# Third attention: its three layer norms applied by ScalarE instead of VectorE, their bias made by GpSimd, second statistics issued behind the division

## The chip, the cores and the metric

One NeuronCore of a Trainium2 chip runs the whole program. The metric is the device time of one execution in microseconds (us). The engines are TensorE (PE, matmuls and weight loads), VectorE (DVE), ScalarE (ACT), GpSimd (POOL) and the DMA queues, which are fed here by SyncE (SP). Each engine takes its own instructions in order; between engines only semaphores order the work.

## What is computed

The network is four residual blocks one after another on 16 sequences of 256 tokens with 128 channels (4096 tokens): a Mamba block, an attention with a mixture of experts, the window attention this change is about, and a two-layer local attention. The third one is

```
x = x + layernorm(attn(layernorm(x)))          # no learned scale or shift in these norms
attn: q, k, v of x; windows of 32 tokens every 16 (8 windows for the 128 + 16 tokens used of a sequence),
      per head of 8 channels scores over the channels' window axis, softmax, output projection W_out
layernorm(x) = (x - mean) / sqrt(var + 1e-5)
```

The local attention that follows starts with a layer norm of this block's result, so the phase ends with yet another norm: for each group of tokens it leaves both x3 = x + norm(attention) and r = norm(x3).

## The kernel before

The program is five phases, each a block with one instruction list per engine; a block ends with a barrier of all engines. The phase of this change is `phase_windows` (from L1953). It has a head and a loop.

**Head.** `x` arrives as 18 tiles of 128 tokens x 128 channels, handled as three sets of six tiles (`norm(k)`, L2192). For each set VectorE takes the statistics (`bn_stats`, `bn_aggr`), adds epsilon into `ve` (L2201), waits for GpSimd, which raises `ve` to the power of -0.5 into `rstd` (L2042), and then applies the norm itself, one `tensor_scalar` per tile, (x - mean) * rstd (L2204). TensorE transposes the normed tiles (`turn_x`, L2057), ScalarE copies them out of PSUM (`copy_x`, L2147), TensorE makes values (`values`) and queries and keys (`queries_keys`), ScalarE copies the values with their bias (`copy_v`), and VectorE adds the bias to queries and keys (`bias(b)`, L2207, 16 sequences). VectorE's written order is norm 0, norm 1, bias 0 to 3, norm 2, bias 4 to 15.

**Loop.** A group is two sequences; there are 8 groups (NG = 8), and each has a turn in which TensorE does, in this order, `weigh(g)` (128 small matmuls of attention weights with values, L2110), `scores(g + 2)` (128 small matmuls, L2094; none for g = 6 and 7) and `project(g)` (L2119, the output projection into the single PSUM bank `y_ps`). `project(g)` waits for two things of VectorE: the transposed heads of its own group (`oT_rd`) and that the bank has been read for the group before (`at_least(pe, y_rd, g)`, L2117).
VectorE's order in the loop is written out by hand (L2287 to L2301):

```
for g in range(NG + 2):
    if g < NG:          turn(g)              # transpose weights, row sums, reciprocal
    if 2 <= g:          first_norm(g - 2)    # yn = (y - mean) * rstd, 4 tiles (L2254)
    if g + 1 < NG:      shift(g + 1)         # add mask, maximum, subtract it
    if 2 <= g:          second_stats(g - 2)  # waits for GpSimd's x3 (L2271)
    if g < NG:          divide(g)            # waits for weigh(g); multiply (L2236), transpose (L2241)
    if 1 <= g <= NG:    take(g - 1)          # reads y_ps (L2260), statistics of y
    if 2 <= g:          second_norm(g - 2)   # ro = (x3 - mean) * rstd, 4 tiles (L2254)
```

ScalarE has only the exponentials here (`exps(g)`, L2166). GpSimd does for each group `rstd1` (L2045), x3 = yn + xr (L2049) and `rstd2` (L2051). SP sends x3 and r of each group out and fetches them into the next phase's tiles. `at_least(engine, semaphore, n)` is a wait that is left out for n = 0; `then_inc` is the signal at an instruction's end; `ln.mark` and `ln.settle` are VectorE's waits for its own instructions.

Of the kernel before, what the change touches and what calls it, by code (L numbers as in the profile page):

```python
# [14 lines left out]
P = 128  # L15
# [10 lines left out]
def at_least(eng, sem, value):  # L26

    if not isinstance(value, int) or value > 0:
        eng.wait_ge(sem, value)
# [1923 lines left out]
def phase_windows(nc, resident, old, signals, x2_dram, x3_dram, r_dram, t):  # L1953
# [8 lines left out]
    with ExitStack() as ctx:  # L1962
# [3 lines left out]
        mhalf = m.sb("mhalf", [P, 6])  # L1966
        xt = m.sb("xt", [P, NT, C])
        stat, mv = m.sb("stat", [P, 6, 6]), m.sb("mv", [P, 6, 2])
        ve, rstd = m.sb("ve", [P, 6]), m.sb("rstd", [P, 6])
        xn = m.sb("xn", [P, NT, C])  # L1970
        xT = m.sb("xT", [P, NB, WTOK])
        vT = m.sb("vT", [P, NB, WTOK])
# [5 lines left out]
        xr = [m.sb(f"xr{i}", [P, NCH, C]) for i in range(2)]  # L1978
        y = m.sb("y", [P, NCH, C])
        stat1, mv1, stat2, mv2 = (m.sb(n, [P, NCH, k]) for n, k in (("stat1", 6), ("mv1", 2), ("stat2", 6), ("mv2", 2)))  # L1980
        ve1, rstd1, ve2, rstd2 = (m.sb(n, [P, NCH]) for n in ("ve1", "rstd1", "ve2", "rstd2"))
        yn = m.sb("yn", [P, NCH, C])
        xo = [m.sb(f"xo{i}", [P, NCH, C]) for i in range(2)]
        ro = [m.sb(f"ro{i}", [P, NCH, C]) for i in range(2)]
# [16 lines left out]
        def tiles_of(k):  # L2001

            return [16, 17, 0, 1, 2, 3] if k == 0 else list(range(6 * k - 2, 6 * k + 4))
# [5 lines left out]
        with nc.Block() as block:  # L2009
# [26 lines left out]
            @block.gpsimd  # L2036
            def _(pool):
                clear(pool, old)
                pool.wait_ge(w_rd, 1)
                for k in range(3):  # L2040
                    pool.wait_ge(var_rd, k + 1)
                    nc.gpsimd.tensor_tensor(rstd[:, :], ve[:, :], mhalf[:, :], ALU.pow).then_inc(rstd_rd, 1)  # L2042
                for g in range(NG):
                    pool.wait_ge(var1_rd, g + 1)
                    nc.gpsimd.tensor_tensor(rstd1[:, :], ve1[:, :], mhalf[:, 0:NCH], ALU.pow).then_inc(rstd1_rd, 1)  # L2045
                    pool.wait_ge(yn_rd, g + 1)
                    pool.wait_ge(r_in[g % 2], 16 * (g // 2 + 1))
                    at_least(pool, x_out[g % 2], 32 * (g // 2))
                    nc.gpsimd.tensor_tensor(xo[g % 2][:, :, :], yn[:, :, :], xr[g % 2][:, :, :], ALU.add).then_inc(x3_rd, 1)  # L2049
                    pool.wait_ge(var2_rd, g + 1)  # L2050
                    nc.gpsimd.tensor_tensor(rstd2[:, :], ve2[:, :], mhalf[:, 0:NCH], ALU.pow).then_inc(rstd2_rd, 1)  # L2051

            @block.tensor
            def _(pe):
# [90 lines left out]
            @block.scalar  # L2145
            def _(act):
                def copy_x(k):  # L2147
                    for i, tiles in enumerate(banks(k)):
                        act.wait_ge(xT_mm, 2 * k + i + 1)
                        if tiles[0] >= NB:  # L2150
                            ins = nc.scalar.copy(xT[:, :, P:WTOK], t_ps[i][:, 0:2 * P].rearrange("p (b t) -> p b t", t=TAIL))
                        else:
                            ins = nc.scalar.copy(xT[:, tiles[0]:tiles[-1] + 1, 0:P],
                                                 t_ps[i][:, 0:len(tiles) * P].rearrange("p (b t) -> p b t", t=P))
                        ins.then_inc(xT_sb, 1)

                def copy_v(n):
                    b0, b1 = 3 * n, min(3 * n + 3, NB)
                    act.wait_ge(v_mm, n + 1)
                    nc.scalar.activation(vT[:, b0:b1, :].rearrange("p b t -> p (b t)"), (o_ps, y_ps)[n % 2][:, 0:(b1 - b0) * WTOK],  # L2160
                                         ACT.Identity, bias=bv[:, 0:1]).then_inc(v_sb, 1)

                def exps(g):
                    act.wait_ge(sub_rd, g + 1)
                    at_least(act, aT_rd, g)
                    nc.scalar.activation(at[:, :, :], sc[:, :, :], ACT.Exp).then_inc(ex_rd, 1)  # L2166

                act.wait_ge(w_rd, 1)
                copy_x(0)
                copy_v(0)  # L2170
                copy_x(1)
                copy_v(1)
                copy_v(2)
                copy_x(2)
                for n in range(3, 6):
                    copy_v(n)
                for g in range(NG):
                    exps(g)

            @block.vector  # L2180
            def _(dve):
# [10 lines left out]
                def norm(k):  # L2192
                    tiles = tiles_of(k)
                    dve.wait_ge(x_in[k], 16 * (20 if k == 0 else 6))
                    for c, b in enumerate(tiles):
                        ln.mark(dve.bn_stats(stat[:, c, :], xt[:, b, :]))
                    ln.settle(apart=True)
                    for c in range(6):
                        ln.mark(dve.bn_aggr(mv[:, c, :], stat[:, c, :]))
                    ln.settle()  # L2200
                    dve.tensor_scalar(ve[:, :], mv[:, :, 1], EPS, None, ALU.add).then_inc(var_rd, 1)  # L2201
                    dve.wait_ge(rstd_rd, k + 1)
                    for c, b in enumerate(tiles):
                        ins = dve.tensor_scalar(xn[:, b, :], xt[:, b, :], mv[:, c, 0:1], rstd[:, c:c + 1], ALU.subtract, ALU.mult)  # L2204
                    ins.then_inc(xn_rd, 1)

                def bias(b):  # L2207
                    dve.wait_ge(qk_mm, b + 1)
# [3 lines left out]
                def shift(g):  # L2212
                    dve.wait_ge(s_mm, g + 1)
                    at_least(dve, ex_rd, g)
                    dve.tensor_tensor(sc[:, :, :].rearrange("p (i j) t -> p i (j t)", i=4), s_all[:, :, 0:P],
                                      off[:, :].unsqueeze(1).to_broadcast([P, 4, P]), ALU.add).then_inc(sc_rd, 1)
                    dve.wait_ge(sc_rd, g + 1)
                    dve.tensor_reduce(nb[:, :], sc[:, :, :], AX.X, ALU.max).then_inc(nb_rd, 1)
                    dve.wait_ge(nb_rd, g + 1)
                    dve.tensor_tensor(sc[:, :, :], sc[:, :, :], nb[:, :].unsqueeze(2).to_broadcast([P, 4 * SQ * 2, WIN]),  # L2220
                                      ALU.subtract).then_inc(sub_rd, 1)
# [18 lines left out]
                    at_least(dve, y_mm, g)  # L2240
                    dve.transpose(oT[:, :, :, :].rearrange("p h k d -> p k h d"), on[:, :, :]).then_inc(oT_rd, 1)  # L2241

                def stats(src, st, mean, dst, done):
                    for c in range(NCH):
                        ln.mark(dve.bn_stats(st[:, c, :], src[:, c, :]))
                    ln.settle(apart=True)
                    for c in range(NCH):
                        ln.mark(dve.bn_aggr(mean[:, c, :], st[:, c, :]))
                    ln.settle()
                    dve.tensor_scalar(dst[:, :], mean[:, :, 1], EPS, None, ALU.add).then_inc(done, 1)  # L2250

                def apply(dst, src, mean, r):
                    for c in range(NCH):
                        ins = dve.tensor_scalar(dst[:, c, :], src[:, c, :], mean[:, c, 0:1], r[:, c:c + 1], ALU.subtract, ALU.mult)  # L2254
                    return ins

                def take(g):
                    dve.wait_ge(y_mm, g + 1)
                    at_least(dve, yn_rd, g)
                    dve.tensor_tensor(y[:, :, :], y_ps[:, :].rearrange("p (c n) -> p c n", c=NCH),  # L2260
                                      bo[:, :].unsqueeze(1).to_broadcast([P, NCH, C]), ALU.add).then_inc(y_rd, 1)
                    dve.wait_ge(y_rd, g + 1)
                    stats(y, stat1, mv1, ve1, var1_rd)

                def first_norm(g):
                    dve.wait_ge(rstd1_rd, g + 1)
                    at_least(dve, x3_rd, g)
                    apply(yn, y, mv1, rstd1).then_inc(yn_rd, 1)

                def second_stats(g):  # L2270
                    dve.wait_ge(x3_rd, g + 1)  # L2271
                    stats(xo[g % 2], stat2, mv2, ve2, var2_rd)

                def second_norm(g):
                    dve.wait_ge(rstd2_rd, g + 1)
                    at_least(dve, x_out[g % 2], 32 * (g // 2))
                    apply(ro[g % 2], xo[g % 2], mv2, rstd2).then_inc(ro_rd, 1)

                norm(0)
                norm(1)  # L2280
# [6 lines left out]
                for g in range(NG + 2):  # L2287
                    if g < NG:
                        turn(g)
                    if 2 <= g:  # L2290
                        first_norm(g - 2)
                    if g + 1 < NG:
                        shift(g + 1)
                    if 2 <= g:
                        second_stats(g - 2)
                    if g < NG:
                        divide(g)
                    if 1 <= g <= NG:
                        take(g - 1)
                    if 2 <= g:  # L2300
                        second_norm(g - 2)  # L2301


    return m.sems
# [860 lines left out]
```

## Time and profile before

| | us |
|---|---|
| median of 3 runs (lowest, highest) | 2429.15 (2426.51, 2434.3) |
| the profiled execution, its own time | 2433.53 |
| its span | 2431.6 |
| TensorE busy | 1976.8 (81%) |
| VectorE busy | 1865.4 (77%) |
| ScalarE busy | 1331.8 (55%) |
| GpSimd busy | 689.4 (28%) |
| mean granted TensorE clock | 0.917 |

The phase of the change lies from about 1301 to 1446 us of that span, some 145 us. Times in the rows are microseconds from the span's start, `[2.43 <-issue]` behind a row is idle time of the engine before it and what ended it ("issue": nothing that the profile shows). A row of several instructions (x4) gives their first start and the time from there that they cover. Busy shares are means over the whole program, so the rows that matter are those of this phase.

### The profile page before, as it was taken

How to read it: one execution, taken by the hardware profiler on the slowest of the kernel's cores; microseconds unless marked ns; L12 is line 12 of the kernel's file. 1: busy time of each engine (PE TensorE's matmuls, PEld its weight loads, DVE VectorE, ACT ScalarE, POOL GpSimd, SP SyncE). 2: the span in 40 equal slices, each digit the busy share in tenths (PEclk: the TensorE clock that was granted, in tenths of full speed). 3: DMA queues.
4: the chain of work that ended last, by engine and by line, in shares of the span. 5: the costliest groups of instructions: out<-in, count | busy, mean ns of one | idle time of the engine just before them, and what ended most of it. 6: DMA issues, size and time to landing. Idle time of an engine off the chain costs nothing. (4 is left out here: it accounts for less than half of the span.)

```text
span 2431.6 us, 39165 instructions
## 1 busy us (share of the span) xinstructions
PE 1976.8 (81%) x12768; PEld 1080.7 (44%) x12768; DVE 1865.4 (77%) x4483; ACT 1331.8 (55%) x2870; POOL 689.4 (28%) x598
## 2 busy tenths in 40 slices
PE   5787787786488989876952758999999999999985
PEld 2233332332234444443422425565656556666553
DVE  5999999999567777741235778888886788888865
ACT  5665656764124444433432007787885487878731
POOL 1333334323201222222441143333331233333211
PEclk8999888998779999978985879999999999999997
DMA  8000000000121111103334130000000000000000
GB/s 282 3 1 5 5 5 5 0 5 5 27 81 36 38 40 39 40 23 107 97 103 135 47 122 1 1 1 1 1 1 1 1 1 1 1 1 2 1 13 22
DMA packets 76458, 79.20 MB, mean 33 GB/s; under 512 B 10004, under 2 KB 60735, under 8 KB 75264
## 3 DMA queue, kind: packets, MB, share of 16 engines
q1 hardware_dynamic: 72160, 68.64, 9.6%
q0 software_dynamic: 4096, 8.06, 1.0%
q8 instruction: 104, 1.70, 0.3%
q14 instruction: 98, 0.80, 0.1%
HBM read 39.19 MB, written 37.85 MB: 32 GB/s over the span
## 5 line engine op out<-in xcount | busy, mean ns | idle before, releaser
L768 DVE TENSOR_TENSOR_SCAN m_hs<-m_da,m_bu 128x1024 f32<-128x1024 f32 x128 | 304.6, 2419 | 0.3
L465 PE MATMUL m_ps_y_ps<-m_prod,m_ident 128*128 128x512 f32 x512 | 278.8, 672 | 4.9 <-DVE m_prod L778 4.9
L1324 ACT ACTIVATE a_pt<-a_ps_s 128x1024 f32<-128x1024 f32 x128 | 131.0, 1024 | 230.1 <-PE a_ps_s L1102 230.1
L375 POOL TENSOR_TENSOR m_bu<-m_dtu,m_bsb 128x1024 f32<-128x1024 f32 x64 | 151.3, 2364 | 366.2 <-ACT m_bsb L616 233.3
L2795 ACT ACTIVATE l_pe<-l_ps_s,l_nbias,l_qs 128x192 f32<-128x192 f32 (+1 forms) x512 | 244.4, 487 | 14.1 <-DVE l_nbias L2963 12.1
L1441 DVE TENSOR_REDUCE a_mpad<-a_ps_s 128x4 f32<-128x1024 f32 x128 | 156.8, 1225 | 94.3 <-PE a_ps_s L1094 93.1
L1094 PE MATMUL a_ps_s<-a_heads 32*128 32x256 f32 x1024 | 188.0, 447 | 45.3 <-DVE a_mpad L1441 29.0
L1102 PE MATMUL a_ps_s<-a_qm,a_heads 32*128 32x256 f32 x1024 | 186.3, 441 | 1.6 <-ACT a_pt L1324 1.2
L2551 PE MATMUL l_ps_s<-l_kT,l_qT 128*128 128x384 f32 (+1 forms) x512 | 180.2, 434 | 0.0
L625 ACT ACTIVATE m_da<-m_dt,m_a_neg 128x510 f32<-128x510 f32 x256 | 167.9, 714 | 3.2 <-DVE m_hs L768 1.7
L465 PEld LDWEIGHTS m_ps_y_ps<-m_prod,m_ident 128*128 128x128 f32 x512 | 113.2, 221 | 113.9 <-issue 97.2
L2805 ACT COPY l_pT<-l_ps_t 128x256 f32<-128x256 f32 (+1 forms) x256 | 122.7, 479 | 72.9 <-PE l_ps_t L2561 45.8
L778 DVE TENSOR_TENSOR m_prod<-m_hs,m_ps_c_ps 128x1024 f32<-128x1024 f32 x128 | 153.9, 1203 | 10.1 <-PE m_ps_y_ps L465 9.7
L616 ACT COPY m_bsb<-m_ps_b_ps 128x512 f32<-128x512 f32 x64 | 37.4, 584 | 209.3 <-PE m_ps_b_ps L451 209.1
L2515 PE MATMUL l_ps_qk<-t_wqkv,l_hT 128*128 128x512 f32 x256 | 145.4, 652 | 1.8 <-ACT l_hT L2755 0.8
L1094 PEld LDWEIGHTS a_ps_s<-a_heads 32*128 32x128 f32 x1024 | 82.3, 193 | 131.5 <-PE a_ps_s L1102 60.3
L2975 DVE TENSOR_SCALAR l_pn<-l_pe,l_ri 128x192 f32<-128x192 f32 (+1 forms) x512 | 132.3, 300 | 10.0 <-DVE l_ri L2971 1.2
L456 PE MATMUL m_ps_c_ps<-m_bc,m_sel 96*128 96x512 bf16 x128 | 54.9, 430 | 99.1 <-DVE m_prod L778 99.1
L2960 DVE TENSOR_REDUCE l_top<-l_ps_s 128x2 f32<-128x256 f32 (+1 forms) x256 | 123.9, 484 | 12.0 <-PE l_ps_s L2551 8.6
L2579 PE MATMUL l_ps_o<-l_pT,l_v 128*64 128x128 f32 x1024 | 113.3, 297 | 12.5 <-ACT l_oT L2811 9.8
L2561 PE MATMUL l_ps_t<-t_ident,l_pn 128*128 128x128 f32 x512 | 100.1, 277 | 26.5 <-DVE l_pn L2975 26.5
L1028 POOL TENSOR_TENSOR a_rstd<-a_ve,a_mhalf 128x2 f32<-128x2 f32 x48 | 33.8, 704 | 306.6 <-DVE a_ve L1399 164.8
(330 smaller groups left out, 4706.2 us busy)
## 6 DMA issues: line engine op xcount, KB each, us to landing
slots<-m_void SPq DMA_DIRECT2D x16, 516.0 KB, 6.3
e_xs<-slots SPq DMA_DIRECT2D x16, 258.0 KB, 2.8
ys<-m_void SPq DMA_DIRECT2D x8, 512.0 KB, 6.7
qk<-a_qk SPq DMA_DIRECT2D x16, 256.0 KB, 2.0
a_heads<-qk SPq DMA_DIRECT2D x64, 64.0 KB
ew_w<-in_w SPq DMA_DIRECT2D x2, 2048.0 KB, 12.5
e_yy<-ys SPq DMA_DIRECT2D x16, 256.0 KB, 5.3
m_xt<-in_L_attn_x SPq DMA_DIRECT2D x8, 256.0 KB, 3.2
```

The source lines that it names most:

```text
L375: nc.gpsimd.tensor_tensor(bu[s % 4][:, :, :], dtu[p][:, :, :], b2, ALU.mult).then_inc(bu_rd, 1)
L465: last = pe.matmul(y_ps[h][:, :], ident[:, :], prod[s % 2][:, h, :], start=False, stop=(s == NS - 1))
L625: nc.scalar.activation(da[s % 4][:, h, :, 1:], dt[p][:, h, :, 1:], ACT.Exp, scale=a_neg[:, h, s:s + 1]).then_inc(da_rd, 1)
L768: dve.tensor_tensor_scan(hs[s % 2][:, :, :].rearrange("p h t -> p (h t)"), da[s % 4][:, :, :, :].rearrange("p h q t -> p (h q t)"), bu[s % ...
L778: dve.tensor_tensor(prod[s % 2][:, :, :], hs[s % 2][:, :, :], c2, ALU.mult).then_inc(prod_rd, 1)
L1094: last = pe.matmul(dst[:, j, :], qT[p][r, g, c * P:(c + 1) * P], kT[p][r, g, :], start=True, stop=True)
L1102: last = pe.matmul(s2[:, j, :], kT[p][r, g, c * P:(c + 1) * P], qm[p][r, g, :], start=True, stop=True)
L1441: dve.tensor_reduce(dst, src[:, :, :], AX.X, ALU.max, negate=True).then_inc(max_rd, 1)
L2515: pe.matmul(qk_ps[:, x, :], hT[:, c * P:(c + 1) * P], t.wqkv[n][:, x * INNER:(x + 1) * INNER], start=True, stop=True).then_inc(l.x_mm[x], 1)
L2551: pe.matmul(both, qT[p][:, j, c * P:(c + 1) * P], kT[p][:, :, j, k0:k0 + nk], start=False, stop=True).then_inc(l.s_mm, 1)
L2795: nc.scalar.activation(pe_[u % 2][:, h, 0:nk], s_ps[u % 2][:, h * 192:h * 192 + nk], ACT.Exp, bias=nbias[:, u % 2, h:h + 1], scale=qs[b % ...
L2975: ins = dve.tensor_scalar(pn[u % 2][:, h, 256 - nk:256], pe_[u % 2][:, h, 0:nk], ri[:, h:h + 1], None, ALU.mult)
```

## The change

GpSimd makes, beside each `rstd`, the product `sh` = (-mean) * rstd, with one more small multiply that waits for the power before it. VectorE writes -mean (`nm`) next to `ve` and no longer applies any norm. ScalarE applies all three norms as Identity with a scale and a bias for each partition, one activation per tile: six per set in the head, four per group for the first and for the second norm. In the head it does so in the order norm 0, copy 0, norm 1, values 0, copy 1, norm 2, values 1 and 2, copy 2. In the loop it does first norm of g - 2, exponentials of g + 1, second norm of g - 2. VectorE's loop becomes turn, shift, divide, second_stats, take. New waits protect the single buffers: GpSimd's power waits for ScalarE's use of the one before, VectorE's statistics wait for GpSimd's use of the mean.

```diff
@@ GpSimd
                 for k in range(3):
                     pool.wait_ge(var_rd, k + 1)
+                    at_least(pool, xn_rd, k)
                     nc.gpsimd.tensor_tensor(rstd[:, :], ve[:, :], mhalf[:, :], ALU.pow).then_inc(rstd_rd, 1)
+                    pool.wait_ge(rstd_rd, 2 * k + 1)
+                    nc.gpsimd.tensor_tensor(sh[:, :], nm[:, :], rstd[:, :], ALU.mult).then_inc(rstd_rd, 1)
                 for g in range(NG):
                     pool.wait_ge(var1_rd, g + 1)
+                    at_least(pool, yn_rd, g)
                     nc.gpsimd.tensor_tensor(rstd1[:, :], ve1[:, :], mhalf[:, 0:NCH], ALU.pow).then_inc(rstd1_rd, 1)
+                    pool.wait_ge(rstd1_rd, 2 * g + 1)
+                    nc.gpsimd.tensor_tensor(sh1[:, :], nm1[:, :], rstd1[:, :], ALU.mult).then_inc(rstd1_rd, 1)
                     pool.wait_ge(yn_rd, g + 1)
...
                     pool.wait_ge(var2_rd, g + 1)
+                    at_least(pool, ro_rd, g)
                     nc.gpsimd.tensor_tensor(rstd2[:, :], ve2[:, :], mhalf[:, 0:NCH], ALU.pow).then_inc(rstd2_rd, 1)
+                    pool.wait_ge(rstd2_rd, 2 * g + 1)
+                    nc.gpsimd.tensor_tensor(sh2[:, :], nm2[:, :], rstd2[:, :], ALU.mult).then_inc(rstd2_rd, 1)
@@ ScalarE
+                def normalise(dst, src, scale, shift, n):
+                    for c in range(n):
+                        ins = nc.scalar.activation(dst[c], src[c], ACT.Identity, bias=shift[:, c:c + 1], scale=scale[:, c:c + 1])
+                    return ins
+
+                def norm_x(k):
+                    act.wait_ge(rstd_rd, 2 * (k + 1))
+                    tiles = tiles_of(k)
+                    normalise([xn[:, b, :] for b in tiles], [xt[:, b, :] for b in tiles], rstd, sh, 6).then_inc(xn_rd, 1)
+
+                def first_norm(g):
+                    act.wait_ge(rstd1_rd, 2 * (g + 1))
+                    at_least(act, x3_rd, g)
+                    normalise([yn[:, c, :] for c in range(NCH)], [y[:, c, :] for c in range(NCH)], rstd1, sh1, NCH).then_inc(yn_rd, 1)
+
+                def second_norm(g):
+                    p = g % 2
+                    act.wait_ge(rstd2_rd, 2 * (g + 1))
+                    at_least(act, x_out[p], 32 * (g // 2))
+                    normalise([ro[p][:, c, :] for c in range(NCH)], [xo[p][:, c, :] for c in range(NCH)], rstd2, sh2, NCH).then_inc(ro_rd, 1)
...
                 act.wait_ge(w_rd, 1)
+                norm_x(0)
                 copy_x(0)
+                norm_x(1)
                 copy_v(0)
                 copy_x(1)
+                norm_x(2)
                 copy_v(1)
                 copy_v(2)
                 copy_x(2)
                 for n in range(3, 6):
                     copy_v(n)
-                for g in range(NG):
-                    exps(g)
+                exps(0)
+                for g in range(NG + 2):
+                    if 2 <= g:
+                        first_norm(g - 2)
+                    if g + 1 < NG:
+                        exps(g + 1)
+                    if 2 <= g:
+                        second_norm(g - 2)
@@ VectorE, head
                     ln.settle(apart=True)
+                    at_least(dve, rstd_rd, 2 * k)
                     for c in range(6):
                         ln.mark(dve.bn_aggr(mv[:, c, :], stat[:, c, :]))
                     ln.settle()
+                    dve.tensor_scalar(nm[:, :], mv[:, :, 0], -1.0, None, ALU.mult)
                     dve.tensor_scalar(ve[:, :], mv[:, :, 1], EPS, None, ALU.add).then_inc(var_rd, 1)
-                    dve.wait_ge(rstd_rd, k + 1)
-                    for c, b in enumerate(tiles):
-                        ins = dve.tensor_scalar(xn[:, b, :], xt[:, b, :], mv[:, c, 0:1], rstd[:, c:c + 1], ALU.subtract, ALU.mult)
-                    ins.then_inc(xn_rd, 1)
@@ VectorE, loop: stats() likewise gains the wait, nm1 or nm2; apply(), first_norm() and second_norm() go
                 for g in range(NG + 2):
                     if g < NG:
                         turn(g)
-                    if 2 <= g:
-                        first_norm(g - 2)
                     if g + 1 < NG:
                         shift(g + 1)
+                    if g < NG:
+                        divide(g)
                     if 2 <= g:
                         second_stats(g - 2)
-                    if g < NG:
-                        divide(g)
                     if 1 <= g <= NG:
                         take(g - 1)
-                    if 2 <= g:
-                        second_norm(g - 2)
```

## Rows read from the trace of the kernel before

**Rows 1.** Windows view, one loop turn: us, busy per engine (count), clock, DMA share, GB/s
```profile
1387.50:1398.00 10.50, 7.72 (x265) 4.47 (x265) 10.05 (x36) 0.63 (x1) 3.33 (x4) 0.83 0.41 128
```
**Rows 2.** Timeline, PE, turns 1 to 3: start, us, engine, line, op, names, count [idle]
```profile
1361.63 1.25 PE L2110 MATMUL w_ps_o<-w_vT,w_aT 32*32 32x32 f32 x126
...
1371.72 1.25 PE L2110 MATMUL w_ps_o<-w_vT,w_aT 32*32 32x32 f32 x126
...
1376.47 0.42 PE L2094 MATMUL w_ps_s<-w_qk 32*32 32x32 f32 x31 [2.64 <-issue]
...
1376.82 5.25 PE L2119 MATMUL w_ps_y<-aw_xn,w_oT 128*128 128x512 f32 x8
...
1381.99 1.25 PE L2110 MATMUL w_ps_o<-w_vT,w_aT 32*32 32x32 f32 x126
```
**Rows 3.** Timeline, DVE: the division of turn 1, then part of turn 3
```profile
1363.02 0.69 DVE L2236 TENSOR_TENSOR w_on<-w_ps_o,w_ri 128x512 f32<-128x512 f32 x1 [4.15 <-PE w_ps_o L2110]
...
1382.11 0.86 DVE L2245 BATCH_NORM_STATS2 w_stat<-w_xo 128x6 f32<-128x128 f32 x4
...
1383.60 0.69 DVE L2236 TENSOR_TENSOR w_on<-w_ps_o,w_ri 128x512 f32<-128x512 f32 x1
...
1384.96 0.65 DVE L2260 TENSOR_TENSOR w_y<-w_ps_y,aw_xn 128x512 f32<-128x512 f32 x1
...
1387.04 0.17 DVE L2250 TENSOR_SCALAR w_ve<-w_mv 128x4 f32<-128x4 f32 x1
```
**Rows 4.** Timeline, PE and DVE, turns 6 and 7
```profile
1412.78 1.29 PE L2110 MATMUL w_ps_o<-w_vT,w_aT 32*32 32x32 f32 x128
...
1415.38 0.69 DVE L2236 TENSOR_TENSOR w_on<-w_ps_o,w_ri 128x512 f32<-128x512 f32 x1
...
1416.75 0.65 DVE L2260 TENSOR_TENSOR w_y<-w_ps_y,aw_xn 128x512 f32<-128x512 f32 x1
...
1417.55 5.35 PE L2119 MATMUL w_ps_y<-aw_xn,w_oT 128*128 128x512 f32 x8 [3.48 <-DVE w_y L2260]
...
1422.82 1.29 PE L2110 MATMUL w_ps_o<-w_vT,w_aT 32*32 32x32 f32 x128
...
1425.31 0.69 DVE L2236 TENSOR_TENSOR w_on<-w_ps_o,w_ri 128x512 f32<-128x512 f32 x1
```
**Rows 5.** Timeline, DVE and POOL, from the last turn to the end of the phase
```profile
1431.27 1.26 POOL L2049 TENSOR_TENSOR w_xo<-w_yn,w_xr 128x512 f32<-128x512 f32 x1 [1.23 <-DVE w_yn L2254]
...
1432.57 0.87 DVE L2245 BATCH_NORM_STATS2 w_stat<-w_xo 128x6 f32<-128x128 f32 x4 [1.38 <-POOL w_xo L2049]
...
1434.03 0.69 DVE L2260 TENSOR_TENSOR w_y<-w_ps_y,aw_xn 128x512 f32<-128x512 f32 x1
...
1442.65 1.11 DVE L2254 TENSOR_SCALAR w_ro<-w_xo,w_mv,w_rstd 128x128 f32<-128x128 f32 x4 [1.13 <-POOL w_rstd L2051]
```
**Rows 6.** Timeline, head of the phase: set 0, then set 2 and queries and keys
```profile
1313.60 0.17 DVE L2201 TENSOR_SCALAR w_ve<-w_mv 128x6 f32<-128x6 f32 x1
1313.92 1.32 POOL L2042 TENSOR_TENSOR w_rstd<-w_ve,w_mhalf 128x6 f32<-128x6 f32 x1 [18.38 <-DVE w_ve L2201]
1315.28 1.63 DVE L2204 TENSOR_SCALAR w_xn<-w_xt,w_mv,w_rstd 128x128 f32<-128x128 f32 x6 [1.51 <-POOL w_rstd L2042]
...
1329.23 0.17 DVE L2201 TENSOR_SCALAR w_ve<-w_mv 128x6 f32<-128x6 f32 x1
...
1329.63 5.55 PE L2079 MATMUL w_ps_s<-aw_xn,w_xT 128*128 128x256 f32 x24
...
```
**Rows 7.** Timeline, ACT, phase before: four tiles with scale and bias
```profile
1295.78 1.65 ACT L1810 ACTIVATE e_yy<-e_yy,e_shift,e_rstd 128x128 f32<-128x128 f32 x4 [1.71 <-DVE e_shift L1927]
```
**Rows 8.** Source views of L2045, L358 (min/median/max ns), and DVE beside L358
```profile
L2045 POOL TENSOR_TENSOR w_rstd<-w_ve,w_mhalf x8: 1007/1042/1045, 1366.7 to 1436.4; 128x4 f32<-128x4 f32 x8
...
L358 POOL TENSOR_TENSOR m_shift_in<-m_nmean,m_rstd x8: 199/3897/3906, 6.6 to 461.5; 128x4 f32<-128x4 f32 x8
...
310.09 4.46 DVE L768 TENSOR_TENSOR_SCAN m_hs<-m_da,m_bu 128x1024 f32<-128x1024 f32 x2
```

More of the change, by code:

```diff
@@ L1968, in phase_windows @@
         stat, mv = m.sb("stat", [P, 6, 6]), m.sb("mv", [P, 6, 2])
-        ve, rstd = m.sb("ve", [P, 6]), m.sb("rstd", [P, 6])
+        ve, rstd, sh = (m.sb(n, [P, 6]) for n in ("ve", "rstd", "sh"))
+        nm, nm1, nm2 = m.sb("nm", [P, 6]), m.sb("nm1", [P, NCH]), m.sb("nm2", [P, NCH])
         xn = m.sb("xn", [P, NT, C])
@@ L1980, in phase_windows @@
         stat1, mv1, stat2, mv2 = (m.sb(n, [P, NCH, k]) for n, k in (("stat1", 6), ("mv1", 2), ("stat2", 6), ("mv2", 2)))
-        ve1, rstd1, ve2, rstd2 = (m.sb(n, [P, NCH]) for n in ("ve1", "rstd1", "ve2", "rstd2"))
+        ve1, rstd1, sh1, ve2, rstd2, sh2 = (m.sb(n, [P, NCH]) for n in ("ve1", "rstd1", "sh1", "ve2", "rstd2", "sh2"))
         yn = m.sb("yn", [P, NCH, C])
@@ L2241, in divide, with stats @@
                     dve.transpose(oT[:, :, :, :].rearrange("p h k d -> p k h d"), on[:, :, :]).then_inc(oT_rd, 1)
-                def stats(src, st, mean, dst, done):
+                def stats(g, src, st, mean, less, dst, done, used):
                     for c in range(NCH):
@@ L2246, in stats @@
                     ln.settle(apart=True)
+                    at_least(dve, used, 2 * g)
                     for c in range(NCH):
@@ L2249, in stats @@
                     ln.settle()
+                    dve.tensor_scalar(less[:, :], mean[:, :, 0], -1.0, None, ALU.mult)
                     dve.tensor_scalar(dst[:, :], mean[:, :, 1], EPS, None, ALU.add).then_inc(done, 1)
[L2252 to L2255, printed above, removed]
                 def take(g):
@@ L2262, in take @@
                     dve.wait_ge(y_rd, g + 1)
[L2263 to L2268, printed above, removed]
+                    stats(g, y, stat1, mv1, nm1, ve1, var1_rd, rstd1_rd)
                 def second_stats(g):
                     dve.wait_ge(x3_rd, g + 1)
[L2272 to L2277, printed above, removed]
+                    stats(g, xo[g % 2], stat2, mv2, nm2, ve2, var2_rd, rstd2_rd)
                 norm(0)
```

## The prediction

> **What bounds the kernel now.** The share of busy time says little here, since this phase is 145 of 2432 us. I read first the windows view, one window per turn of the loop: a turn lasts 10.5 us and VectorE is busy for 10.05 of it [rows 1]. That invites the reading that VectorE is the bound and that whatever is taken from it is gained. The timeline of TensorE says otherwise. The weighs of turns 1, 2 and 3 start at 1361.63, 1371.72 and 1381.99, so 10.09 and 10.27 us apart [rows 2], and in the first of these two intervals VectorE sat idle for 4.15 us waiting for the weigh [rows 3]: with VectorE plainly not the limit, the pitch was already the same. What fills it is TensorE's own list: the weigh of 1.25 us, the scores with a hole of 2.64 us that no semaphore explains, and the projection of 5.25 us at 1376.82, which ends as the next weigh starts [rows 2]. Through turn 5 VectorE (10.5 us a turn) runs just behind TensorE (10.1 to 10.3) and eats its slack without yet stopping it. Only in turns 6 and 7, which have no scores, does TensorE wait for VectorE: the projection starts at 1417.55 behind 3.48 us of idling, released by VectorE's read of the bank `y_ps` [rows 4]. After turn 7 the phase is one serial chain through VectorE and GpSimd to the last second norm [rows 5], and in the head everything stands behind the first normed set [rows 6].
>
> So there are four places: head, turns 2 to 5, turns 6 and 7, tail.
>
> **Prices of the new pieces.** ScalarE's norm of four tiles: the same operation on the same shape, Identity with scale and bias, took 1.65 us in the phase before [rows 7], and I take 1.65 for four, 0.41 a tile, 2.48 for six. VectorE needs 1.11 us for four and 1.63 for six [rows 5, 6]. GpSimd's multiply of 128x4 exists in the Mamba phase, from 0.20 us up to 3.90, the long ones under VectorE's scans [rows 8]. The single operations of VectorE in these rows take 0.7 us at most, and in the tail it waits while GpSimd multiplies, so I take 0.20 plus 0.08 for the step from the power, the gap seen from `ve` to the power; 3.90 stays as the upper end. The extra `nm` on VectorE: between 0.02 and the 0.17 us of its twin `ve` [rows 3]; as neighbours on VectorE start before the one before is reported done, I take 0.09. A handover from GpSimd to ScalarE is priced as that from GpSimd to VectorE, 0.04 [rows 6].
>
> A rule speaks against the move. The Trainium skill, page "ScalarE: Activation LUTs", in its closing table of situations, gives add and multiply to VectorE, up to about three times faster there in bf16. The trace has the same direction but 1.5 times for fp32. With that factor of three instead, a four-tile norm would cost 3.3 us, and the estimate below would grow by about 1.7 for each of three norms and 2.4 for the head, to about 12 us.
>
> **Head.** Before, from the end of `ve` (1313.77) to the end of set 0's norm (1316.91) it is 3.14 us [rows 6]. After: 0.15 to the power, 1.32, then 0.28 for the multiply, 0.04, and 2.48 on ScalarE, 4.27 in all: +1.1 us, and TensorE's transposes wait for the last tile. From there to the scores TensorE's list is nearly unbroken, so the delay reaches the loop; a few tenths may return, because VectorE no longer norms set 2 while banks wait to be read, and these I leave to the lower edge. ScalarE's `norm_x(2)` stands ahead of `copy_v(1)` and `copy_v(2)`, but those have no user before set 2 is transposed: with `ve` of set 2 at 1329.40 + 1.1 and 4.27 behind it, the norm ends at about 1334.8, and TensorE is done with queries and keys 4 to 9 at 1335.18 + 1.1 [rows 6]. The work beside it hides it. Head: +1.1.
>
> **Turns 2 to 5.** VectorE loses 2 x 1.11 us of norms and gains 2 x 0.09. This frees VectorE, not TensorE. But the new order has a cost of its own: `take`, whose first instruction reads the bank that `project(g)` waits for, now stands behind the second statistics, which stand behind the division. Counted from a weigh's start: the division starts 1.39 later [rows 2, 3], the transpose and it take 1.36 to the next instruction (1383.60 to 1384.96), the statistics 1.46 (1432.57 to 1434.03) [rows 3, 5] and `nm` 0.09, so the bank's read starts at 4.30; 0.65 to read and 0.15 to reach TensorE [rows 4] give 5.10. Before, the projection started 5.10 after its weigh [rows 2]. The wait is thus just hidden by the hole in the scores: 0, at most 0.1 a turn. Are the second statistics' inputs there? `take` ends 2.25 + 0.09 after 4.30, at 6.64. Then 0.08 + 1.04 power [rows 8], 0.28 multiply, 0.04, 1.65 ScalarE, 0.08 + 1.26 GpSimd's add and 0.04: 4.47, so x3 is there at 11.11, which is 0.9 after the next weigh, and is wanted at 2.75. Slack 1.85. ScalarE has the exponentials between its two norms; it is free by then. Sum: +0.05.
>
> **Turns 6 and 7.** The division came late, 2.60 and 2.49 after the weigh instead of 1.39 [rows 4], and that is repaired. It gives nothing, since the projection waits for the bank: before, the bank was read straight after the division and the projection started 4.77 after weigh 6 [rows 4]; now it is 5.10. Weigh 7 comes +0.33 later. Turn 7 loses the like, but that is covered by the tail's own wait.
>
> **Tail.** `take(7)` stands behind the second statistics of group 6, as before. Their input comes 11.11 after weigh 7 by the chain above, and 1.55 later the bank is read: 12.66. Before it was 1434.03 - 1422.82 = 11.21 [rows 4, 5]: +1.45. The projection itself is done at about 10.5, so it hides nothing. Behind it both norms of group 7 are serial: twice 0.28 for the multiply, 0.09 for `nm` and 1.65 - 1.11 = 0.54 for ScalarE, +1.8. The output DMA, SP's two fetches and the barrier follow the last norm, so all of it reaches the end.
>
> **Sum:** 1.1 + 0.05 + 0.33 + 1.45 + 1.8 = 4.7 us slower. The profiled execution took 2433.53 (span 2431.6); it would take 2438. It lay 4.4 above the median of the runs, 2429.15, from which I forecast 2433.9. That is 0.19%, below the 0.3% (7.3 us) which is about what a measurement of this kernel can tell from no change. With the multiply at 0.2 to 0.7 and `nm` at 0.02 to 0.17 the case spans +3.5 to +8, and with the spread of the runs shown 2430 to 2439.
>
> **Rivals.**
> (1) *VectorE is the bound after all, and the loop gets its time back.* For it: 10.05 of 10.5 us busy, and the late divisions. Then turns 2 to 7 gain 2.22 - 0.18 = 2.04 each, 12.2 us, against 1.1 + 1.45 + 1.8: 8 us faster, 2421. It decides if TensorE's turn can be under 10.1, that is if the hole in its scores shrinks and the bank's wait too. Against it stands the pitch of 10.09 beside 4.15 us of VectorE idling, and the new cycle weigh, division, second statistics, read, projection, which is 5.10 + 5.2 whatever else is gained. Chance 0.07.
> (2) *The multiply on GpSimd is held up by VectorE.* In the Mamba phase the same multiply took 3.90 us while two scans of VectorE ran over it [rows 8]. The Trainium skill, "GPSIMD Engine Reference", Key points, says that GpSimd shares its SBUF interfaces with VectorE and contends with VectorE's two-input or two-port instructions. Here the subtraction in `shift` is of that kind, once a turn. The case decides when the multiply takes over 0.2 + 1.85 us: then x3 is late, VectorE waits in the second statistics, the bank is read late and TensorE's projection with it. At 3.90 that is 3.70 - 1.85 = 1.85 in each of turns 2 to 7, 11.1 us, and 3.7 in the head: +19, 2448, slower. Against it: the eight powers of the first norms stay between 1.01 and 1.05 us [rows 8], beside a busy VectorE as beside an idle one, and no scan runs. Chance 0.08.
> (3) *The change's parts cancel.* If the hand-overs and the multiply are all at their lower ends and the head's delay is caught up by TensorE before the loop, 1 to 2 us remain, 2431. It is the lower edge of my case, inside its chance.
>
> **Numbers.** My case has 0.85, of which about a fifth reaches over +7.3 us (bank wait of 0.1 to 0.3 in every turn, or handovers to ScalarE dearer than to VectorE). Faster: 0.07. Slower: 0.08 + 0.17 = 0.25. Same: 0.68. The range leaves out rival 1 and most of rival 2: 2428.5 to 2440.5.
>
> **What would show it.** In the changed trace: the first transposes about 1.1 us later; pitch of the weighs in turns 2 to 5 unchanged within 0.2 while VectorE now idles one to two us a turn; the projections of turns 6 and 7 released by L2260's counterpart at about 5.1 after their weighs; the read of the bank for group 7 at about 12.7 after weigh 7; the phase 4 to 5 us longer. A pitch under 10 us would prove the sum wrong on one side, GpSimd multiplies of over 1 us on the other.

## The result and the profile after

| | before | after |
|---|---|---|
| median of 20 runs each (lowest, highest), us | 2428.76 (2422.19, 2434.88) | 2436.72 (2429.23, 2440.45) |
| ratio, 95% interval | | 1.0026 (1.0018 to 1.0034), so +4.4 to +8.3 us |
| the phase of the change, VectorE's first instruction in it to its first in the next | 144.5 | 149.1 |
| VectorE busy, ScalarE busy, GpSimd busy, us | 1865.4, 1331.8, 689.4 | 1846.3, 1364.8, 694.8 |

The forecast was +4.7 us, 2433.9, within the 0.3% that counts as no change; measured is +6.3 by the ratio (the medians lie 8.0 apart). VectorE lost 19 us of work and the program became slower. The two profiled executions differ by less, 1.2 us in their spans, because in the second the phases ahead of this one happened to take 3.2 us less; so the whole is read from the 20 runs and the phase from its own start. In the changed kernel the weigh is L2120, the projection L2129, the division L2274, the bank's read L2295, ScalarE's norms L2175.

The windows view of one turn of the changed kernel, columns as in [rows 1]:
```profile
1385.00:1395.50 10.50, 8.00 (x265) 4.54 (x265) 8.34 (x31) 3.92 (x9) 4.01 (x6) 0.83 0.40 129
```
VectorE is busy 8.34 us of the turn where it was 10.05 [rows 1]; TensorE's 8.00 stands against 7.72. The turn did not get shorter. The timeline of turns 5 to 7 answers to [rows 2] and [rows 4]:
```profile
1400.43 1.25 PE L2120 MATMUL w_ps_o<-w_vT,w_aT 32*32 32x32 f32 x126
...
1405.51 5.32 PE L2129 MATMUL w_ps_y<-aw_xn,w_oT 128*128 128x512 f32 x8 [0.45 <-DVE w_y L2295]
...
1410.76 1.29 PE L2120 MATMUL w_ps_o<-w_vT,w_aT 32*32 32x32 f32 x128
...
1412.15 0.69 DVE L2274 TENSOR_TENSOR w_on<-w_ps_o,w_ri 128x512 f32<-128x512 f32 x1 [1.66 <-PE w_ps_o L2120]
...
1415.28 0.68 DVE L2295 TENSOR_TENSOR w_y<-w_ps_y,aw_xn 128x512 f32<-128x512 f32 x1
...
1416.11 5.14 PE L2129 MATMUL w_ps_y<-aw_xn,w_oT 128*128 128x512 f32 x8 [4.07 <-DVE w_y L2295]
...
1421.18 1.29 PE L2120 MATMUL w_ps_o<-w_vT,w_aT 32*32 32x32 f32 x128
```
VectorE now waits for the weigh (1.66 us), and the division starts 1.39 after it. But the projection starts 5.08 (turn 5) and 5.35 (turn 6) after its weigh, released by the bank's read. The head and the tail, answering to [rows 6] and [rows 5]:
```profile
1310.49 0.16 DVE L2243 TENSOR_SCALAR w_ve<-w_mv 128x6 f32<-128x6 f32 x1
1310.81 1.32 POOL L2044 TENSOR_TENSOR w_rstd<-w_ve,w_mhalf 128x6 f32<-128x6 f32 x1 [18.45 <-DVE w_ve L2243]
...
1312.21 0.20 POOL L2046 TENSOR_TENSOR w_sh<-w_nm,w_rstd 128x6 f32<-128x6 f32 x1
1312.50 2.42 ACT L2175 ACTIVATE w_xn<-w_xt,w_sh,w_rstd 128x128 f32<-128x128 f32 x6 [18.27 <-POOL w_sh L2046]
...
1315.06 1.51 PE L2073 MATMUL w_ps_t<-aw_ident,w_xn 128*128 128x128 f32 x6 [65.77 <-ACT w_xn L2175]
...
1432.18 0.87 DVE L2283 BATCH_NORM_STATS2 w_stat<-w_xo 128x6 f32<-128x128 f32 x4 [4.42 <-POOL w_xo L2056]
...
1433.72 0.68 DVE L2295 TENSOR_TENSOR w_y<-w_ps_y,aw_xn 128x512 f32<-128x512 f32 x1
...
1437.24 0.20 POOL L2052 TENSOR_TENSOR w_sh<-w_nm,w_rstd 128x4 f32<-128x4 f32 x1
...
1437.47 1.65 ACT L2175 ACTIVATE w_yn<-w_y,w_sh,w_rstd 128x128 f32<-128x128 f32 x4 [0.60 <-POOL w_sh L2052]
```
From the end of `ve` to the first transpose it is 4.41 us. Before it was 3.28, from 1313.77 [rows 6] to this row of the timeline before:
```profile
1317.05 1.51 PE L2063 MATMUL w_ps_t<-aw_ident,w_xn 128*128 128x128 f32 x6 [64.65 <-DVE w_xn L2204]
```
From weigh 7 to the last read of the bank it is 12.54 (11.21 before).

### The profile page after: what moved, and what is told of

It reads as the page before. It is cut to its first block and busy times, and to the rows that moved or that the text cites. A ratio compares the mean times of both kernels' runs of the same rounds, so it can differ in the third digit from the quotient of the medians.

```text
span 2432.8 us, 39219 instructions
## 1 busy us (share of the span) xinstructions
PE 1977.9 (81%) x12768; PEld 1080.7 (44%) x12768; DVE 1846.3 (76%) x4420; ACT 1364.8 (56%) x2952; POOL 694.8 (29%) x617
```

## The experiments

Single executions differ by some microseconds, and the first and third of the three sets below ran on chips on which every kernel takes about 2460. So the phase is read from each trace in pieces: end of `ve` to first transpose; VectorE's start to the first scores; weigh 1 to 6; weigh 6 to the end of the phase; and of that, weigh 7 to the bank's last read, and that read to the end. "Weigh 1 to 6" is turns 1 to 5. A piece is a difference of starts in the timeline. The stretch from the scores to weigh 1 is not in the table: it took 16.8 us before and 18.0 after the change in the first pair, but 18.4 in both repeats, and 16.8 to 18.4 with either kind of head where the scores are whole. As far as these traces show, it differs from execution to execution and not by the change.

| kernel | phase | ve to transpose | start to scores | weigh 1 to 6 | weigh 6 to end | weigh 7 to read | read to end |
|---|---|---|---|---|---|---|---|
| before | 144.5 | 3.28 | 43.6 | 51.2 | 32.9 | 11.21 | 11.7 |
| before, again (e11) | 144.6 | 3.28 | 42.3 | 51.5 | 32.3 | 11.20 | 11.7 |
| after | 149.1 | 4.41 | 43.0 | 51.8 | 36.3 | 12.54 | 13.4 |
| after, again (e9) | 148.1 | 4.41 | 44.2 | 49.2 | 36.3 | 12.54 | 13.4 |
| order only (e1) | 146.2 | 3.28 | 42.7 | 51.9 | 33.6 | 11.58 | 11.7 |
| read early (e2) | 143.7 | 4.40 | 44.2 | 48.1 | 33.0 | 10.09 | 15.5 |
| read early, again (e12) | 147.8 | 4.40 | 44.5 | 53.4 | 33.1 | 10.09 | 15.5 |
| head on VectorE (e3) | 148.3 | 3.28 | 42.3 | 52.0 | 36.1 | 12.54 | 13.4 |
| VectorE filled (e4) | 151.2 | 4.40 | 44.6 | 53.2 | 36.3 | 12.55 | 13.4 |
| half scores, after (e5) | 147.6 | 4.40 | 44.3 | 51.0 | 36.6 | 12.55 | 13.4 |
| half scores, read early (e6) | 136.8 | 4.39 | 44.5 | 40.9 | 35.2 | 9.62 | 15.5 |
| half scores, before (e10) | 141.5 | 3.28 | 42.5 | 50.7 | 32.9 | 11.22 | 11.7 |
| tail on VectorE (e7) | 146.0 | 4.40 | 44.4 | 49.2 | 33.9 | 11.74 | 11.8 |
| combined (e8) | 142.6 | 3.28 | 42.2 | 51.7 | 30.5 | 8.80 | 12.8 |

**The new order alone (e1).** The kernel before, with `divide(g)` moved ahead of `second_stats(g - 2)` as in the change's diff, norms left on VectorE.

> The kernel before with nothing but VectorE's new order: the second statistics behind the division, all norms still on VectorE. Length of the phase is taken from VectorE's first instruction in it to its first in the next phase: 144.5 us before, 149.1 after the change. My theory: the order costs, since the bank is now read about 5.0 us after each weigh; turns 2 to 5 stay at 10.2 to 10.5 us, project 6 starts about 5.0 after weigh 6 (4.7 to 4.8 before, 5.35 after the change), and the division of turn 6 starts 1.4 after its weigh only if VectorE keeps up. Phase 144.5 to 146. Rival (VectorE's lateness in the division was the cost, the order repairs it): phase 142 or less.

Phase 146.2, just over the 144.5 to 146 expected; projections at 5.16 to 5.17 in turns 3 to 6, ratio 1.0012 (0.9991 to 1.0032). The order alone repairs nothing: weigh 6 to end is 33.6 against 32.3 and 32.9.

**The bank read ahead of the second statistics (e2, e12).** The changed kernel with

```diff
                     if g < NG:
                         divide(g)
+                    if 1 <= g <= NG:
+                        take(g - 1)          # only the read of y_ps
                     if 2 <= g:
                         second_stats(g - 2)
                     if 1 <= g <= NG:
-                        take(g - 1)
+                        take_stats(g - 1)
```

> The changed kernel with the read of the bank (first instruction of take) put between the division and the second statistics, its statistics left where they are. My theory (TensorE waits for that read in turns 6 and 7, and in the tail it stands behind the second statistics of group 6): projects 6 and 7 start about 3.6 us after their weighs instead of 5.35 and 5.07, weigh 7 comes 1.5 us sooner, the tail gains 0.6 more; phase 149.1 - 2.2 = about 147. Turns 2 to 5 unchanged at 10.2 to 10.4. Rival (the wait is not the bank, or the loss is elsewhere): phase 149.

> The early read of the bank once more: project 3.55 after the weigh in turns 6 and 7 and weigh 6 to the end of the phase 33.0 us, against 36.3 for the changed kernel; phase 144 to 147, ratio to the kernel before 1.000 to 1.001.

```profile
1432.83 1.29 PE L2120 MATMUL w_ps_o<-w_vT,w_aT 32*32 32x32 f32 x128
...
1436.37 3.67 PE L2129 MATMUL w_ps_y<-aw_xn,w_oT 128*128 128x512 f32 x8 [2.26 <-DVE w_y L2295]
1440.31 1.29 PE L2120 MATMUL w_ps_o<-w_vT,w_aT 32*32 32x32 f32 x128 [0.26 <-DVE w_aT L2264]
```
The timeline of turn 6 in e2: the projection starts 3.54 after its weigh, as expected in both runs. Weigh 6 to the end falls by 3.3 and not 2.2: the eight matmuls take 3.67 us where they took 5.14 in the changed kernel. In the windows view the granted clock of turn 6 is 1.00 of full speed here (2.4 GHz throughout) and 0.84 there, where TensorE had idled 4.07 us before them instead of 2.26; e8 below shows that the short wait alone does not give this clock. Of the tail's gain only 0.4 us arrives of the 0.6 expected, since weigh 7 now comes so soon that in its turn VectorE waits 0.36 us for group 5's x3:
```profile
1444.07 0.87 DVE L2283 BATCH_NORM_STATS2 w_stat<-w_xo 128x6 f32<-128x128 f32 x4 [0.36 <-POOL w_xo L2056]
...
1450.40 0.69 DVE L2295 TENSOR_TENSOR w_y<-w_ps_y,aw_xn 128x512 f32<-128x512 f32 x1 [3.17 <-ACT w_yn L2175]
...
1451.67 0.87 DVE L2283 BATCH_NORM_STATS2 w_stat<-w_xo 128x6 f32<-128x128 f32 x4 [0.58 <-POOL w_xo L2056]
```
The last read itself waits for ScalarE's first norm of group 6, because there is one buffer `y`, but VectorE idles another 0.58 us behind it for x3, so this wait costs nothing. The phases, 143.7 and 147.8, missed the 147 and the 144 to 147 expected, one on each side, through the loop: over weigh 1 to 6 the same kernel took 48.1 and 53.4. So the whole (ratios 1.0003, 0.9984 to 1.0021, and 1.0007, 0.9985 to 1.0029) does not set it apart from the kernel before.

**The head back on VectorE (e3).** `norm_x` removed from ScalarE, six `tensor_scalar` back in `norm(k)`, no `sh` in the head.

> The changed kernel with the head's three norms back on VectorE as before, the loop as changed. My theory: TensorE's first transposes start 3.3 us after ve of set 0 instead of 4.4; if that delay of 1.1 us really reaches the loop the phase is 148; the first weigh of the loop moves with TensorE's clock by up to 2 us, so this is read from the distance from ve to the first transpose. Rival (TensorE's clock in the head, not the norm, sets when the loop starts): the phase stays at 149 within 1 us either way.

3.28 us again, and the start of the scores at 42.3 against 44.2 in e9. The phase, 148.3, fits the theory (148) and the rival (149 within 1) alike and does not decide between them. The ratio is 1.0015 (0.9999 to 1.0032).

**VectorE filled up again (e4).** Four `tensor_scalar` of 128x128 into a scratch tile ahead of the division, turns 2 to 7.

> The changed kernel with four more tile operations of VectorE (about 1.1 us, as one of the norms it lost) in turns 2 to 7 ahead of the division, into a scratch tile. My theory (VectorE's freed time buys nothing): VectorE's wait for the weigh shrinks by 1.1 us a turn, the pitch of the weighs stays at 10.3 to 10.4, phase 149 to 150. Rival (VectorE's load is on the path): 6 x 1.1 more, phase 155 to 156.

```profile
1430.96 1.70 DVE L2320 TENSOR_SCALAR w_waste<-w_y 128x128 f32<-128x128 f32 x4
1432.75 0.69 DVE L2275 TENSOR_TENSOR w_on<-w_ps_o,w_ri 128x512 f32<-128x512 f32 x1
```
The fill took 1.70 us here and VectorE was still not late: the division starts 1.38 after its weigh (1.38 to 1.39 in every turn from 1 on but turn 3, where it is 1.75), and the pitch in turns 4 to 6 is 10.38, 10.37 and 10.36. Turn 3 of this run took 12.07, with a granted clock of 0.72 in it. The late division accounts for 0.3 to 0.4 us of that, the projection of 6.73 us for the rest; the read-early kernel had such a turn (12.13, 0.72) without any fill. With that turn the phase is 151.2, which lies between the theory's 149 to 150 and the rival's 155 to 156; the pitches of the other turns decide. The whole (ratio 1.0020, 1.0000 to 1.0041) is inconclusive.

**TensorE's list made shorter, three times (e5, e6, e10).** Each leaves out half of the scores' matmuls from group 2 on:

```diff
-                            for q in range(4):
+                            for q in range(2 if 2 <= g else 4):
```

> The changed kernel without half of the matmuls of the scores from group 2 on (64 a turn left out, so the scores of half the heads' rows are stale). Theory A (in the changed kernel TensorE waits for the bank in every turn as soon as its own list gets shorter): project stays at 5.07 after the weigh, pitch 10.2 to 10.4 in turns 2 to 5, and TensorE's idle time is then put down to VectorE's read instead of to issue. Theory B (only TensorE's own list sets the pitch): project starts 0.5 us or more sooner, pitch under 9.9.

> The early read of the bank together with half of the scores' matmuls left out from group 2 on (64 a turn). Theory A (bank read behind the second statistics closes a cycle of 5.07 + 5.2 us): with that read early the cycle is open, so project starts 3.6 to 4.2 after its weigh in turns 2 to 5 and the pitch falls to 9.5 or less. Rival (something else, as VectorE's load, holds 10.3): pitch 10 or more.

> The kernel before without half of the scores' matmuls from group 2 on (64 a turn left out). If VectorE, busy 10.05 us a turn with the norms, is a second bound right behind TensorE, the pitch stays at 10.1 to 10.5 and project then waits for VectorE. If VectorE had room, the pitch falls under 9.9.

The timeline of TensorE in turn 4 of e5, then its waits over turns 2 to 6 (us in total, times, longest):
```profile
1392.31 5.37 PE L2129 MATMUL w_ps_y<-aw_xn,w_oT 128*128 128x512 f32 x8 [3.23 <-DVE w_y L2295]
```
```profile
PE w_ps_y L2129 <- DVE w_y L2295: 14.5, 5, 4.1
```
With 64 matmuls fewer a turn the projection of the changed kernel stays at 5.08 and the pitch at 10.37: what was a hole in the scores is now a wait for the bank. With the read early (e6) the same cut brings weigh 1 to 6 down to 40.9 us, 8.2 a turn. Part of that is the clock, which was 1.00 in turns 1, 3 and 5; but turns 2 and 4, at 0.81 and 0.82, took 8.85 and 9.73, also under 10.37. (Turn 4, with 4.44 from weigh to projection, lies outside what was expected.) So the changed order closes a cycle of 5.07 + 5.3 us. The kernel before (e10) has another bound at the same place; the timeline of its reads of the bank:
```profile
1401.58 0.65 DVE L2260 TENSOR_TENSOR w_y<-w_ps_y,aw_xn 128x512 f32<-128x512 f32 x1
...
1412.09 0.65 DVE L2260 TENSOR_TENSOR w_y<-w_ps_y,aw_xn 128x512 f32<-128x512 f32 x1
...
1422.59 0.65 DVE L2260 TENSOR_TENSOR w_y<-w_ps_y,aw_xn 128x512 f32<-128x512 f32 x1
```
They are 10.51 and 10.50 apart: VectorE goes its 10.5 us a turn, while TensorE's pitches swing from 7.4 to 13.1 and are 10.1 on the mean of turns 1 to 5.

**Both runs again (e9, e11).** Unchanged kernels, to see what repeats.

> The changed kernel once more, to see what of its phase repeats. Both theories: the terms that VectorE, ScalarE and GpSimd set repeat within 0.1 us (ve to first transpose 4.4, weigh 7 to the read of the bank 12.5, read to the next phase 13.4, projects 6 and 7 at 5.07 to 5.35); what TensorE's granted clock sets (first transpose to weigh 1, length of a projection) may differ by up to 2 us; phase 148 to 151.

> The kernel before once more, to see how much of its phase repeats: terms set by VectorE and GpSimd within 0.1 us (weigh 7 to the read of the bank 11.2, read to the next phase 11.7, ve to first transpose 3.3), the stretches set by TensorE's clock within 2 us; phase 143 to 146.

The terms of VectorE, ScalarE and GpSimd repeat within 0.02 us; what TensorE's clock sets moves by up to 2.6 (weigh 1 to 6: 51.8 and 49.2). The ratio of the changed kernel in this set was 1.0017 (1.0004 to 1.0029).

**The tail back on VectorE (e7).** Norms of groups 6 and 7 as `tensor_scalar`, no `sh` for them.

> The changed kernel with both norms of groups 6 and 7 back on VectorE and without GpSimd's multiply for them. My theory (the tail is a serial chain in which each norm on ScalarE costs 0.54 us for ScalarE's tiles and 0.28 for the multiply): three norms lie on the chain, weigh 7 to the read of the bank falls from 12.5 to 11.7, read to the next phase from 13.4 to 11.7; phase 149.1 - 2.5 = 146.6. Rival (the tail is set elsewhere, by TensorE or by the DMAs): nothing moves.

```profile
1434.25 1.03 POOL L2050 TENSOR_TENSOR w_rstd<-w_ve,w_mhalf 128x4 f32<-128x4 f32 x1 [1.24 <-DVE w_ve L2303]
1435.32 1.12 DVE L2309 TENSOR_SCALAR w_yn<-w_y,w_mv,w_rstd 128x128 f32<-128x128 f32 x4
```
The norm follows the power directly: 11.74 and 11.8, as expected; 2.4 us less behind weigh 6, of 2.5 expected. Ratio to the kernel before 1.0002 (0.9990 to 1.0013).

**What the parts add up to (e8).** Norms on ScalarE for groups 0 to 5, on VectorE in the head and for 6 and 7; read early; in the tail the statistics of group 7 before the second ones of group 6:

```diff
+                tail_first(6)
+                take(7)
+                take_stats(7)
+                second_stats(6)
+                tail_first(7)
+                tail_second(6)
+                second_stats(7)
+                tail_second(7)
```

> The loop of the changed kernel for groups 0 to 5 with the early read of the bank, VectorE's norms in the head and for groups 6 and 7, and in the tail the statistics of group 7 ahead of the second statistics of group 6. My theory: head 1.1 us less than after the change, turns 6 and 7 as in the early read (project at 3.55 after the weigh and at full clock, pitch 7.5), tail 21 us from weigh 7 to the next phase instead of 25.9; phase 138 to 141, 4 to 6 us under the kernel before, ratio about 0.998. Rival: the clock or the DMAs take it back, phase over 143.

Ratio 0.9986 (0.9976 to 0.9997): faster than the kernel before by 1 to 6 us, and the median, 2426.11, lies 7.2 under that of the changed kernel in the same set. The phase is 142.6 and misses the 138 to 141, without reaching the rival's 143. The projection of turn 6 started at 3.55 as expected but ran at a clock of 0.81 and took 5.37, turn 2 had a pitch of 11.07, and the tail from weigh 7 took 21.6 instead of 21:
```profile
1432.00 1.26 POOL L2064 TENSOR_TENSOR w_xo<-w_yn,w_xr 128x512 f32<-128x512 f32 x1
1432.06 2.06 DVE L2305 TENSOR_SCALAR w_ro<-w_xo,w_mv,w_rstd 128x128 f32<-128x128 f32 x4
```
VectorE's four tiles, 1.11 us elsewhere [rows 5], took 2.06 beside GpSimd's add, and the second statistics of group 7 came behind them. The projections of turns 6 and 7 followed the same wait and ran at different clocks, 0.81 and 1.00:
```profile
1412.92 5.37 PE L2139 MATMUL w_ps_y<-aw_xn,w_oT 128*128 128x512 f32 x8 [2.26 <-DVE w_y L2317]
...
1421.77 3.67 PE L2139 MATMUL w_ps_y<-aw_xn,w_oT 128*128 128x512 f32 x8 [2.26 <-DVE w_y L2317]
```

## Why the prediction was right

**The reading it started from.** One row was read wrongly. The 4.15 us of VectorE's idling end with the division of turn 1 at 1363.02, so they begin at 1358.87, and only the last 1.39 of them lie between weighs 1 and 2, where the prediction puts them all. The windows view of that interval in the kernel before:
```profile
1361.63:1371.72 10.09, 7.72 (x265) 4.42 (x265) 8.39 (x26) 0.59 (x1) 2.28 (x2) 0.83 0.06 21
```
VectorE was busy 8.39 of 10.09 us, so it had 1.7 us of room and not 4.15. The conclusion, that VectorE did not set this turn, stands; that its relief buys nothing in the later turns is shown by e4, e5 and e6 and not by this row, which the prediction uses again against rival 1.

**Prices.** ScalarE's norm, 1.65 for four and 2.42 for six; multiply 0.20 in all its places (198 to 200 ns over the eight of L2052); `nm` 0.08 (1415.13 to 1415.21 in the timeline) for 0.09. All hit, and the factor of three, which would have given +12 us, is refuted here: fp32 tiles of 128x128 cost ScalarE 1.5 times VectorE's time.

**Head: +1.1.** The step itself is +1.13. What arrives at the scores is more: over the kernels of the table with ScalarE's head the start of the scores lies at 44.2 on the mean (8 kernels, 43.0 to 44.6), with VectorE's at 42.6 (6 kernels, 42.2 to 43.6), so 1.6. The granted clock has a part in this. Between first transpose and scores it was 0.85 to 0.86 in all but one of the first kind and 0.89 to 0.90 in all but one of the second. At about 0.90 the start is 43.0 against 42.2 to 42.7, at 0.85 it is 44.2 to 44.6 against 43.6: at equal clock the change costs 0.6 to 0.7, less than the term of 1.1, and the lower clock costs 1.2 to 1.4 more. Each of these comparisons has a single kernel on one side. Whether the change brings the lower clock with it, and why, is open. In the first pair of traces the clock was the other way round (0.90 after, 0.85 before), and that hid the term (43.0 against 43.6).

**Turns 2 to 5: 0.** Right: 51.8 and 49.2 us over weigh 1 to 6 against 51.2 and 51.5. The projection started 5.07 to 5.08 after its weigh in all of turns 3 to 5, for the 5.10 of the sum. The prediction had this wait just hidden by the hole in the scores; in turn 5 it ended last, by 0.45 us, as the row above shows. What it costs a turn is less than executions differ by: turns 3 to 5 of the changed kernel took 10.25 to 10.38, and with the bank read early, at the same clock, it was 9.8 to 10.2 in e2 and, in turns 4 and 5, 10.3 to 10.5 in e12. e5 and e6 show the cycle behind it, e4 that VectorE's freed time buys nothing.

**Turns 6 and 7: +0.33.** Weigh 6 to 7 took 10.42 and 10.38 against 10.04 and, in e11, 9.46: +0.4 to +0.9. That the first pair comes so near the term is in part luck: the projection started 5.35 after weigh 6 and not 5.10 (4.77 before, 4.16 in e11), and its matmuls took 5.14 where they had taken 5.35. The prediction said nothing of the clock in these turns. In e2 and e12 the projections that waited less also ran faster, 3.67 us; that the shorter wait is the cause is not shown, since in e8 turn 6 had it and ran at 0.81.

**Tail: +1.45 + 1.8.** Measured are 12.54 - 11.21 = +1.33 and 13.4 - 11.7 = +1.7, both a little under their terms.

With the head at 1.6 the pieces add up to 1.6 + 0 + 3.4 to 4.0 behind weigh 6 = 5.0 to 5.6, inside both intervals of the ratio. That the phase itself grew by 4.6 in the first pair, so near the 4.7 of the sum, is luck in its parts: the start of the scores moved by -0.6, the stretch from there to weigh 1 by +1.2, turns 1 to 5 by +0.6 and the rest by +3.4.

**Rivals.** (1) fell: no gain in the loop. Its ground was better than the prediction's own turn 1 suggests, though: e10 shows VectorE at 10.5 us a turn as a bound just behind TensorE's list, and the changed kernel put the bank's cycle of 10.3 in its place. Three bounds within about 0.4 us of each other (10.1 to 10.3, 10.5 and 10.3 to 10.4) made the relief of one worthless. (2) fell: the multiply was never held up. (3) that the parts cancel fell as well.

## What to carry to other kernels

Before an engine is relieved, time one turn in which it visibly waits, with the idle time inside that turn: if the pitch is the same there, the relief buys nothing, and the price is paid in the head and tail, where a norm moved to an engine with dearer tiles and one more hand-over is serial. When instructions are reordered, ask for each single PSUM bank who waits for its read, and put that read ahead of work that nobody waits for.

## What was not expected of the hardware

GpSimd's add of 128x512 took 1.26 us alone and 1.46 at the median in the changed kernel, where it now runs beside VectorE's subtraction of two SBUF tiles; the source view and the timeline of the changed kernel:
```profile
L2056 POOL TENSOR_TENSOR w_xo<-w_yn,w_xr x8: 1260/1462/1495, 1367.2 to 1439.2; 128x512 f32<-128x512 f32 x8
```
```profile
1378.26 0.69 DVE L2258 TENSOR_TENSOR w_sc<-w_sc,w_nb 128x512 f32<-128x512 f32 x1
...
1378.58 1.50 POOL L2056 TENSOR_TENSOR w_xo<-w_yn,w_xr 128x512 f32<-128x512 f32 x1 [1.76 <-ACT w_yn L2175]
```
In the tail, where no such subtraction runs, the add takes 1.26 us, as all eight did before the change (1.26 to 1.27). So the rule that the prediction takes from the Trainium skill ("GPSIMD Engine Reference", Key points), that GpSimd contends with VectorE's instructions of two SBUF inputs, fits what the add shows in this phase. No multiply was held up, and the add's 0.2 us fell into slack. It goes the other way too: VectorE's four tiles beside that add took 2.06 us instead of 1.11 in e8, and in e4 1.70 in turns 2 to 6, where the add ran beside them, against 0.56 in turn 7, where it did not. Source views of e4 and e8 (min/median/max ns of one tile) and the timeline of e4's turn 7:
```profile
L2320 DVE TENSOR_SCALAR w_waste<-w_y x24: 163/214/1301, 1397.0 to 1450.1; 128x128 f32<-128x128 f32 x24
```
```profile
L2305 DVE TENSOR_SCALAR w_ro<-w_xo,w_mv,w_rstd x8: 333/340/1290, 1432.1 to 1437.6; 128x128 f32<-128x128 f32 x8
```
```profile
1449.71 0.56 DVE L2320 TENSOR_SCALAR w_waste<-w_y 128x128 f32<-128x128 f32 x4
```
It is one tile that is held and not all four: in e8 the longest took 1.29 us from 1432.06, which puts its end 0.09 us behind the add's.

The hole in the scores is TensorE's largest idle piece of a turn in both kernels, 1.9 to 3.1 us. In turns 0 to 5 it lies ahead of the last 13, 22, 31, 40, 49 and 58 of their 128 matmuls, so 9 matmuls earlier each turn. No experiment here was aimed at it, and its cause is open.

In turns 1 to 7 a projection of eight matmuls took 3.7 us where the granted clock of the turn was 1.00, 5.1 to 5.4 at 0.81 to 0.85, and 5.9 to 6.7 in the four turns at 0.72 to 0.74. Which of these a turn got differed between executions of one kernel (weigh 1 to 6: 48.1 and 53.4 for the read-early kernel), which is more than the 4.6 us by which the change lengthened the phase.
